# Router scores in column strips from unrounded x, and x's transposes by token tile, in a fused attention and mixture-of-experts kernel

## What is computed

```python
xn = _layernorm(x)
qkv = xn @ w_qkv                      # 256 -> 768, 16 heads of 16
q, k = elu(q) + 1, elu(k) + 1
kv_t = decay * kv_{t-1} + k_t * v_t   # per head, over the 1024 tokens
ks_t = decay * ks_{t-1} + k_t
att = (q * kv / max(sum(q * ks), eps)) @ w_out
router_logits = xn @ router_w.T       # 8 experts, the best one is taken
gate = sigmoid(top logit)
routed = down(silu_mul((xn * gate) @ w_gate_up[e]))  # of that expert
shared = down(silu_mul(xn @ shared_gate_up))
return x + att + routed + shared
```

## Time and profile before

| | us |
|---|---|
| median of three runs (129.26 to 131.13) | 129.44 |
| the profiled execution | 129.56 |
| its span in the trace | 127.9 |
| outside the span | 1.7 |
| TensorE busy | 122.5 (96%) |
| VectorE busy | 79.7 (62%) |
| ScalarE busy | 52.4 (41%) |
| GpSimd busy | 35.2 (28%) |

### The profile page before, as it was taken

One profiled execution on the slowest core, in us unless ns is written; L12 is line 12 of the kernel. 1 busy time (PEld: TensorE's weight loads), 2 busy tenths in 40 slices (PEclk: granted clock), 3 DMA queues, 4 the chain that ended last, 5 costly groups with the idle time before them and its releaser, 6 DMA issues.

```text
span 127.9 us, 2432 instructions
## 1 busy us (share of the span) xinstructions
PE 122.5 (96%) x826; PEld 106.6 (83%) x826; DVE 79.7 (62%) x176; ACT 52.4 (41%) x111; POOL 35.2 (28%) x63
## 2 busy tenths in 40 slices
PE   4989999999999999999999999999999999999990
PEld 1258767787888667999999999999999978999990
DVE  0899886999999977755575553515140428922371
ACT  1665796979954725422222222242121337200000
POOL 6804000007888200030303030303030301687500
PEclk9999999999999999999999999999999999999999
DMA  3681999999992210129888988889782031033427
GB/s 95 204 275 60 308 356 243 173 255 399 394 350 109 82 51 0 46 60 293 286 284 290 272 318 264 319 255 336 255 310 75 1 94 51 17 92 96 117 97 243
DMA packets 15748, 25.02 MB, mean 196 GB/s; under 512 B 1296, under 2 KB 12632, under 8 KB 15736
## 3 DMA queue, kind: packets, MB, share of 16 engines
q1 hardware_dynamic: 13368, 20.66, 51.2%
q0 software_dynamic: 1456, 3.41, 8.0%
q10 hardware_dynamic: 912, 0.80, 1.9%
HBM read 18.78 MB, written 6.08 MB: 194 GB/s over the span
## 4 chain that ended last, share of the span: by engine, by line
PE 80%; POOL 6%; issue 5%; DMA 4%; DVE 2%; ACT 0%; DVEq 0%; POOLq 0%
PE ps L1105 25%; PE ps L1119 13%; POOL q_sb L450 6%; PE ps L295 5%; PE ps L296 5%; PE ps L297 5%; PE ps L965 5%; PE ps L971 4%; PE ps L978 4%; PE ps L1049 4%; DMA q_sb<-sorted_rows,slot_row 2%; PE ps L1036 2%; DMA sorted_rows<-yrow 2%; PE ps L1043 2%; DVE x_sb L889 1%
## 5 line engine op out<-in xcount | busy, mean ns | idle before, releaser
L1105 PE MATMUL ps<-xgT,gu 128*128 128x144 f32 x256 | 34.0, 286 | 0.0
L1105 PEld LDWEIGHTS ps<-xgT,gu 128*128 128x128 f32 x256 | 32.3, 190 | 0.3 <-ACT xgT L528 0.2
L820 DVE TENSOR_TENSOR wqkv<-rz,ps 128x288 f32<-128x288 f32 x16 | 7.3, 454 | 25.9 <-ACT rz L564 25.8
L432 POOL DMA_DIRECT2D sorted_rows<-yrow x9 | 5.0, 560 | 55.5 <-DVE yrow L815 55.5
L1119 PE MATMUL ps<-wqkv,dn 128*128 128x144 f32 x128 | 17.4, 289 | 0.0
L564 ACT ACTIVATE rz<-ps 128x288 f32<-128x288 f32 x16 | 6.6, 411 | 25.4 <-PE ps L1105 25.4
L424 POOL DMA_INDIRECT sorted_rows<-xn,slot_row x8 | 11.2, 1396 | 19.0 <-ACT xn L500 17.2
L1119 PEld LDWEIGHTS ps<-wqkv,dn 128*128 128x128 f32 x128 | 16.1, 190 | 0.0
L295 PE MATMUL ps<-xT_hi,sgu_hi 128*128 128x512 f32 x32 | 13.0, 405 | 0.0
L296 PE MATMUL ps<-xT_lo,sgu_hi 128*128 128x512 f32 x32 | 12.5, 390 | 0.0
L297 PE MATMUL ps<-xT_hi,sgu_lo 128*128 128x512 f32 x32 | 12.5, 390 | 0.0
(11 more groups left out here) (162 smaller groups left out, 230.3 us busy)
## 6 DMA issues: line engine op xcount, KB each, us to landing
gu<-in_L_ffn_w_gate_up_dram SPq DMA_DIRECT2D x8, 1024.0 KB
dn<-in_L_ffn_w_down_dram SPq DMA_DIRECT2D x8, 512.0 KB
sorted_rows<-zeros SPq DMA_DIRECT2D x1, 2592.0 KB, 17.8
wqkv<-sorted_rows SPq DMA_DIRECT2D x10, 144.0 KB
sorted_rows<-yrow POOLq DMA_DIRECT2D x9, 128.0 KB, 2.1
sgu<-_ffn_shared_gate_up_dram SPq DMA_DIRECT2D x1, 1024.0 KB, 6.1
wqkv<-in_L_attn_w_qkv_dram SPq DMA_DIRECT2D x3, 256.0 KB, 3.7
x_sb<-in_L_attn_x_dram SPq DMA_DIRECT2D x2, 256.0 KB, 3.7
```

The lines of the kernel that those rows point to most:

```text
L820: V.tensor_tensor(hr[:, 2 * h:2 * h + 2, :].rearrange("p f s -> p (f s)"), act_sb[:, h, 0:2 * SLOTS], ps[:, 2 * h + 1, 0:2 * SLOTS], ALU.m ...
L1105: ins = mm(ps[:, 2 * h + u, (f % 2) * SLOTS:(f % 2 + 1) * SLOTS], gu[p][:, kc, col:col + P], xgT[:, kc, :], start=(kc == 0), stop=(kc == K ...
```

## The change

The two token halves' router products become one step. `router_logits()` makes four fp32 matmuls (token half n, feature half c), each into its own strip of 32 partitions of one bank (`LROW`), from `xT_raw`, the transposed x without rounding; the two feature halves are added by VectorE's first reduction in `choose`. `xT_raw` is written in four pieces: two copies by ScalarE (first token half), one sum hi + lo by GpSimd and one copy by VectorE (second token half). The router weights are no longer split; they are padded with zeros to 32 columns. The scores are transposed by 4 full transposes in place of 8 small ones.

`transpose_tokens` now loops over token tiles outside and feature halves inside, and both halves' semaphores are signalled at the last tile. In the first token half the second feature half is rounded by VectorE. VectorE's `x_lo(0)` stands ahead of two of the statistics, `place()` ahead of `q_sb` of group 1, and the first half of `sgu_lo` ahead of `choose`. `WARM` is 12. Projection tiles use other banks, which changes their waits and those of `shared_tile`. The decay matmuls stand in `ranks`, which stands inside tile 8.

```diff
-WARM = 14
+WARM = 12
+        xT_raw = sb("xT_raw", [P, KC, T], F32)
-        rT = sb("rT", [P, KC, 2, E], F32R)
+        rT = sb("rT", [P, KC, STRIP], F32)
+        LROW = 4
+        ROUTE = 5
+        qkv_bank = [0, 1, 2, 3, 7, 6, 0, 1, 2, 3, 4, 7]
+        logit_ps = ps[:, ROUTE, :].rearrange("p (i c e) -> p e i c", c=KC, e=STRIP)[:, 0:E]
-        gate_bank = [4, 0, 2, 4, 0, 2, 4, 2]
+        gate_bank = [0, 2, 4, 0, 2, 0, 4, 2]
-        bank_user = {3: 0, 4: 1, 5: 2, 6: 3}
+        bank_user = {3: 0, 4: 1, 5: 3, 6: 2}
...
+            pool.wait_ge(s_xlo, KC + 1)
+            pool.tensor_tensor(xT_raw[:, 0, 512:], xT_hi[:, 0, 512:].bitcast(F32), xT_lo[:, 0, 512:].bitcast(F32), ALU.add).then_inc(s_xraw_pool, 1)
...
             def x_hi(n):
-                for c in range(KC):
+                for c in range(n + 1):
...
+            for c in range(KC):
+                act.wait_ge(s_xlo, c + 1)
+                A(xT_raw[:, c, 0:512], ps[:, 4 + c, :], ACT.Copy).then_inc(s_xraw_act, 1)
             act.wait_ge(s_var, 2)
...
+                    if t in (2, 5):
+                        c = t // 3
+                        act.wait_ge(s_sgu, 16)
+                        A(sgu_hi[:, c, :], sgu[:, c, :], ACT.Copy).then_inc(s_shi, 1)
                     if t == 2:
...
-                        act.wait_ge(s_lrow, NH)
-                        A(lrow[:, 1, :], ps[0:2 * E, ROUTE, :], ACT.Copy).then_inc(s_lcopy, 1)
-                    if t in (2, 5):
...
+                        act.wait_ge(s_lrow, 1)
+                        A(lrow, ps[:, LROW, :], ACT.Copy).then_inc(s_lcopy, 1)
...
+            dve.wait_ge(s_xT, KC)
+            V.tensor_copy(xT_hi[:, 1, 0:512], ps[:, 5, :]).then_inc(s_xhi_dve, 1)
+            x_lo(0)
             for i in range(TH, TH + 2):
                 statistics(i)
-            x_lo(0)
...
-            dve.wait_ge(s_lrow, 1)
-            V.tensor_copy(lrow[:, 0, :], ps[0:2 * E, ROUTE, :]).then_inc(s_lcopy, 1)
             x_lo(1)
+            V.tensor_copy(xT_raw[:, 1, 512:], ps[:, 5, :]).then_inc(s_xraw_dve, 1)
...
-                if a == 0:
-                    dve.wait_ge(s_decp, 1)
-                    V.tensor_copy(decay[:, :], ps[:, 7, 256:256 + KC]).then_inc(s_decay, 1)
-                dve.wait_ge(s_er, 2 * a + 2)
-                V.scalar_tensor_tensor(q_sb[:, c, cols], ps[:, (3 * a + 2) % 4, :], 1.0, ez[:, 1, :], ALU.add, ALU.max).then_inc(s_q, 1)
-                if a == 0:
-                    choose()
                 if a == 1:
                     place()
+                dve.wait_ge(s_er, 2 * a + 2)
+                V.scalar_tensor_tensor(q_sb[:, c, cols], ps[:, qkv_bank[3 * a + 2], :], 1.0, ez[:, 1, :], ALU.add, ALU.max).then_inc(s_q, 1)
+                if a == 0:
+                    weight_lo(0)
+                    choose()
                 if a == KC:
-                    for h in range(KC):
-                        dve.wait_ge(s_shi, h + 1)
-                        V.tensor_tensor(sgu_lo[:, h, :], sgu[:, h, :], sgu_hi[:, h, :].bitcast(F32), ALU.subtract).then_inc(s_slo, 1)
+                    weight_lo(1)
...
+                for j in (0, 3, 1, 2):
...
+                    for c in range(KC):
+                        ins = tr(ps[:, 4 + c, j * P:(j + 1) * P], xn[:, n * TH + j, c * P:(c + 1) * P], ident[:, :])
+                        if j == 2:
+                            ins.then_inc(s_xT, 1)
+
+            def router_logits():
+
+                pe.wait_ge(s_rhi, 1)
+                pe.wait_ge(s_xraw_pool, 1)
+                pe.wait_ge(s_xraw_dve, 1)
+                for g in range(NH * KC):
+                    n, c = g // KC, g % KC
+                    ins = mm(ps[g * STRIP:(g + 1) * STRIP, LROW, :], rT[:, c, :], xT_raw[:, c, n * 512:(n + 1) * 512], start=True, stop=True)
+                ins.then_inc(s_lrow, 1)
...
-            for t in range(3):
+            for t in range(4):
                 qkv_tile(t)
-            router_logits(0)
             transpose_tokens(1)
-            qkv_tile(3)
-            router_logits(1)
...
             qkv_tile(4)
+            qkv_tile(5)
+            router_logits()
+            qkv_tile(6)
             transpose_logits()
```

More of the change, by code:

```diff
@@ L380, in _ @@
             pool.memset(spread[:, :, :], 1.0).then_inc(s_const, 1)
+            pool.memset(rT[:, :, :], 0.0).then_inc(s_rclear, 1)
             pool.wait_ge(s_const, 5)
@@ L739, in k_scan, with weight_lo @@
                                      ksum[:, c, cols.start - 1:cols.start] if a >= KC else 0.0, ALU.mult, ALU.add).then_inc(s_ks, 1)
+            def weight_lo(h):
+                dve.wait_ge(s_shi, h + 1)
+                V.tensor_tensor(sgu_lo[:, h, :], sgu[:, h, :], sgu_hi[:, h, :].bitcast(F32), ALU.subtract).then_inc(s_slo, 1)
             for a in range(2 * NH):
@@ L914, in router_logits @@
-            def router_logits(n):
-                pe.wait_ge(s_rlo, 1)
-                if n:
-                    pe.wait_ge(s_lcopy, 1)
-                cols = slice(n * 512, (n + 1) * 512)
-                both = ps[0:2 * E, ROUTE, :]
-                pe.wait_ge(s_xhi, 2 * n + 2)
-                for c in range(KC):
-                    mm(both, rT[:, c, :, :].rearrange("p h e -> p (h e)"), xT_hi[:, c, cols], start=(c == 0), stop=False, skip_group_check=True)
-                for c in range(KC):
-                    pe.wait_ge(s_xlo, 2 * n + c + 1)
-                    ins = mm(both[0:E, :], rT[:, c, 0, :], xT_lo[:, c, cols], start=False, stop=(c == KC - 1), skip_group_check=True)
+                    pe.wait_ge(s_xraw_act, KC)
@@ L936, in transpose_logits @@
                 ins.then_inc(s_logit, 1)
             def ranks():
+                pe.wait_ge(s_dech, 1)
                 pe.wait_ge(s_chosen, 1)
+                for c in range(KC):
+                    mm(ps[:, ROUTE, 256 + c:257 + c], spread[:, c, :], dec_h[:, :], start=True, stop=True)
                 pick = chosen[:, :, :].rearrange("p e i -> p (e i)")
@@ L981, in qkv_tile @@
                 hi_hi()
+                if t == 8:
+                    ranks()
                 if t == 0:
@@ L1055, in _ @@
             transpose_tokens(0)
-            for t in range(3):
+            for t in range(4):
                 qkv_tile(t)
-            router_logits(0)
             transpose_tokens(1)
-            qkv_tile(3)
-            router_logits(1)
-            pe.wait_ge(s_dech, 1)
-            pe.wait_ge(s_rlo, 1)
-            for c in range(KC):
-                ins = mm(ps[:, 7, 256 + c:257 + c], spread[:, c, :], dec_h[:, :], start=True, stop=True)
-            ins.then_inc(s_decp, 1)
             qkv_tile(4)
+            qkv_tile(5)
+            router_logits()
+            qkv_tile(6)
             transpose_logits()
-            qkv_tile(5)
-            qkv_tile(6)
-            ranks()
             for t in range(7, 12):
```

78 lines of the change are left out of this document (38 added, 40 removed).

## The result

The changed kernel takes 131.20 us (median of 6 runs, 130.85 to 132.33); the kernel before took 129.56 beside it (6 runs, 129.26 to 131.13). The ratio is 1.013 with a 95% interval of 1.009 to 1.017. That is 1.58 above the profiled execution of the kernel before, where 1.05 was forecast.

A forecast was written before the change was run, and what follows sets the result against it. VectorE's chain was held as critical as TensorE's, arriving at `head_sums` within 0.1 us. ScalarE's delayed run adds 1.05: 129.56 + 1.05 = 130.6, on the median's scale 130.5 us; 8-in-10 range 128.8 to 131.4.

The forecast's parts named there:

- the case that it called likeliest: ScalarE's q of group 2 waits for VectorE's q_sb, moving everything by 1.05 us; 129.9 to 131.1, chance 0.62.
- GpSimd's sum: Second token half: hi + lo for the unrounded x starts at 16.97, takes 1.30 us, ends at 18.27.
- the start: First half: `xn` sets it, not the warm-up; tile 0 at 8.64, tile 2's end earlier, gain 0.34 us.
- ScalarE's run to `hidden(0)`: From tile 8's relu through exp, scaling and first silu, gapless before; all moves by 1.05 us, hidden at 36.43.
- the new copy: Second half on VectorE, behind the two `x_lo(1)` differences: starts at 17.43, takes 0.60 us.
- TensorE's own gain: TensorE alone: router steps 1.83 less strips 0.99 plus earlier start 0.34, about 1.2 us, up to 1.6.
- the idle time forecast ahead of `head_sums`: TensorE finishes the tile ahead of `head_sums` at 43.7 and waits 1.7 us there.
- (1): ScalarE's wait costs nothing and VectorE alone decides; `head_sums` 0.1 to 0.4 earlier, 129.0 to 129.4 us; chance 0.20.
- (2): TensorE alone decides the time: -1.2 to -1.6, 127.9 to 128.3 us; chance 0.06.
- (3): Unrounded x reaches the router late: GpSimd's sum at twice 1.30 gives +1.3, 131.8 us; chance 0.09.
- (4): TensorE's clock falls to 1.2 GHz over tiles 0 to 3 with the shorter warm-up; up to 135 us; chance 0.03.
- The rule weighed: VectorE instructions with two SBUF inputs and GpSimd SBUF reads exclude each other; none holds up GpSimd's sum, forecast stays 130.5.

The follow-up runs named there:

- e1: `after` with place() put back behind q_sb of group 1, nothing else; 130.28 us, ratio 1.007 to the kernel before.
- e2: The kernel before with place() moved ahead of q_sb of group 1, nothing else; 130.80 us, ratio 1.008.
- e10: `after` with GpSimd's subtraction for the q weights waiting for VectorE's for the v weights; 130.88 us, ratio 1.008.
- `after`: The changed kernel itself, with the whole change, against the kernel before; 131.20 us, ratio 1.013.
- e6: e5 with the second half of sgu_lo made by GpSimd in place of VectorE; 130.14 us, ratio 1.004.
- e8: e6 with ScalarE's scaling in three parts (1, 2 and 5 token tiles, the last behind the first silu); 129.93 us, ratio 1.003.
- experiment 6: Test of VectorE's and GpSimd's subtractions holding one another up: one GpSimd wait added to `after` (130.88 us) and to e8 (129.76 us).
- e4: `after` with ScalarE's scaling of five token tiles moved behind the first silu; 130.36 us, ratio 1.005.
- e12: `after` with transposes by feature half as in the kernel before; 131.97 us, ratio 1.014.
- e5: `after` with the edits of e1 and e4 joined; 130.91 us, ratio 1.011.
- e9: `after` with WARM = 14; 131.87 us, ratio 1.018.
- e3: `after` with WARM = 8; 132.99 us, ratio 1.028.
- e7: The kernel before with ScalarE's scaling of five token tiles moved behind the first silu; 129.99 us, ratio 0.999.

## Why the prediction was right, and where its size was off

**The forecast held**: 130.5 with a range of 128.8 to 131.4 against 131.2, and the case that it called likeliest is the one in the trace. The time lies 0.1 above the band that it gave that case (129.9 to 131.1): the loss was 1.6 us by the medians, and 1.05 had been forecast. `q_sb` of group 1 behind `place` holds up ScalarE's relu of tile 8, what is queued behind it on ScalarE moves as one piece, and TensorE's gain becomes idle time. e1 takes that wait out and `head_sums` comes 1.04 earlier, 0.93 of it by the edit. e2 puts the same order into the kernel before, and `head_sums` comes 0.97 later. That the two numbers are alike is chance: in e2 the chain runs over a bank that TensorE waits for, and ScalarE's way is worth some 0.8.

**Step by step**, forecast and measured (start in us, where nothing else is said):

| step | forecast | measured |
|---|---|---|
| tile 0 | 8.64 | 9.01 |
| tile 3 | 13.15 | 13.55 |
| second half rounded by ScalarE | 15.6 | 15.92 |
| GpSimd's sum ends | 18.27 | 18.62 |
| router | 18.37 | 18.72 |
| scores at VectorE | 21.42 | 21.86 |
| `choose` ends | 23.03 | 23.48 |
| relu of tile 8 | 27.56 | 27.95 |
| `hidden(0)` | 36.43 | 36.81 |
| `head_sums` | 45.40 | 45.76 |

The error is there in the first row and stays between 0.32 and 0.45 down to the last. **The term that was mis-sized is the start**, the 0.34 that the earlier first half was to give: measured, it gave nothing (tile 0 at 9.01 and tile 2's end at 13.55; before, 9.02 and 13.49). Two parts: `x` landed 0.14 later in this execution (VectorE's first statistics at 3.66 for 3.52), and from the end of the last `xn` to ScalarE's rounding it takes 0.56 (7.71 to 8.27), where I had 0.34. e10, in which TensorE stood waiting for `xn`, has 0.52 for that step (7.64 to 8.16), so this is its length and not a delay by the warm-up. I had taken the step from a kernel in which TensorE was late there and `xn` had long been done. Of the rest, 1.41 by `head_sums` becomes 1.5 in the span by 0.09 in the tail, and 0.1 lies outside the span.

**The terms that held**: four strips of fp32 matmuls 0.99 from start to start (18.72 to 19.71; forecast 0.99); GpSimd's sum 1.30; `choose`, `place` and `q_sb` from scores to relu 6.09 (forecast 6.14); ScalarE's run to `hidden(0)` 8.86 (8.87); the new copy 0.60 from start to start. The 0.30 of VectorE's wait for the scores was forecast as 0.27.

**TensorE's own gain**: it comes to the shared expert 1.04 earlier (29.49 for 30.53), by 0.84 from the router steps (1.83 less 0.99) and 0.15 from the transposes of the scores (0.60 to 0.45). The forecast had "about 1.2" in its sum and then 29.0 for 30.69 in its text on the wait, 0.5 more than its own terms give. That was a slip, and 0.16 of it comes of 30.69 being the chain's time for a start that the timeline has at 30.53. The matmuls of the shared tiles also followed one another more slowly than before (11.62 for 11.34 over the last 50), which no term had. So the idle time forecast ahead of `head_sums`, 1.7, was too long: from start to start the trace has 0.94 at `sgu_lo` (1.0 forecast) and 1.05 ahead of `head_sums`. This changed nothing, since VectorE decided.

**The rivals.** (1), that the wait costs nothing, is out: the rows of `after`, and e1. (2), TensorE alone, is out for `after`; e6 and e8 show what it was worth, 44.25 and 44.10 for `head_sums`, not the 43 that its forecast meant, because the start gain was missing, GpSimd became the next link, and the shared matmuls ran slower. (3), the unrounded x late, is out, and the two came as close as forecast: GpSimd's sum ended at 18.62, and the router started at 18.72, 0.56 behind tile 5's last pair where pairs follow at 0.47, so 0.1 at most was lost there. (4), the clock, did not come at 12 warm matmuls and did at 8.

**The rule weighed** was the Trainium skill's (SBUF — State Buffer, Who interferes with whom). By it the sum of `xT_raw` had no collision to fear, and it had none, 1.30. But the rule also covers the pair of `wqkv_lo`, both with two inputs in SBUF, and I did not apply it there, though the change moves one of them by 0.64 towards the other. It is what experiment 6 shows: 1.68 for 0.68 in one order, 1.64 for 1.30 in the other. The forecast could have had this as a rival: up to +1.0 in some executions.

**What stays open.** Why TensorE's shared matmuls take 0.28 longer over 50 of them in the changed program, which is a part of the 0.37 that e1 still loses, is not known; the banks are other ones there, and no run takes them back. That the long executions of `after`, e1, e4 and e12 without a profile are all due to the meeting at 10.8 is inferred from the profiled ones, not seen in each; the kernel before has long ones too (130.97 and 131.13 among its first six), and none of those was profiled.

## What to carry to other kernels

When two engines reach a joint within 0.1 us of one another, work taken off one is worth nothing; ask first which wait ends last there, and of every step that is put behind another, who on a third engine waits for it: here one `q_sb` moved behind 2.3 us of small VectorE steps cost 0.9, whatever TensorE gained. When the same edit costs the same in two kernels, look in both traces whether it takes the same way: in e2 it didn't. Take the length of a hand-over from a place where the receiver was waiting, not from one where it was late. If an edit moves a VectorE instruction with two SBUF inputs, look at what GpSimd does in the new place, in more than one execution: one wait on GpSimd gave both steps their short durations again.

## What the runs showed of the hardware that I had not expected

Two subtractions of 128x512 with both inputs in SBUF, one on VectorE and one on GpSimd, do not run side by side. Started 0.16 us after GpSimd's (10.63, 1.29 long), VectorE's took 1.68 for 0.68; started 0.20 after VectorE's (10.84), GpSimd's took 1.64 for 1.30. Either way the second seems to do most of its work only when the first is through: 11.92 and then 0.55, 11.52 and then 1.16. The same two remainders stand in all nine profiled executions in which the pair met (0.54 or 0.55 for VectorE in e4, e5, e9 and e12; 1.15 or 1.16 for GpSimd in `after`, e3, e6, e7 and e8). In e3 the two began within 0.03 (GpSimd's at 10.80, VectorE's at 10.83), and it was GpSimd's, recorded first, that took 1.85: so close together the recorded start does not tell which one waits. This agrees with the Trainium skill (SBUF — State Buffer, Who interferes with whom). The order, and with it 1.0 us of the kernel's time, hung on whether the q weights had landed so that ScalarE rounded them from 9.9 (e5) or from 10.3 (`after`): VectorE's being late costs TensorE 0.83, GpSimd's being late costs it nothing.

With 8 warm matmuls the granted clock was 0.81 from 8 to 10 us and 0.50 from 10 to 12; TensorE had stood 1.49 us ahead of the transposes. It was full with 12 and with 14. With the same 12 warm matmuls, the instruction behind them (the transposes of the router weights) came at 7.01 in the profiled execution of `after` and at 6.58 in that of e10; the trace names nothing that it waited for.
